# A state space stage whose decays come as running products from one VectorE scan per unit

## The reference, cut to what matters

```python
proj = hidden_states @ W_in.T                    # z | x, B, C | dt
xBC  = silu(causal_conv4(xBC) + conv_b)          # 34 x 128 channels
dt   = softplus(dt + dt_bias);  A = -exp(A_log)
dA   = dt * A                                    # per head and token
Lmat = exp(segsum(dA))                           # L[s,t] = exp(dA[s+1] + ... + dA[t]) for s <= t, else 0
Y_diag = einsum('bclhn,bcshn,bhcls,bcshp->bclhp', C, B, Lmat, x * dt)
y = Y_diag + (states carried over chunks) + D_param * x
g = y * silu(z)
gn = g * rsqrt(mean(g * g) + eps) * norm_w
out = gn @ W_out.T
```

## Time and profile before

| | us |
|---|---|
| median of 3 runs | 4260.26 |
| lowest, highest | 4255.05, 4267.71 |
| span of the profiled execution | 4258.5 |
| this stage, from the first projection of dt to the last layer norm | about 2790 to 3905 |
| distance of two units inside a group | 7.68 |

### The profile page before, as it was taken

The page is one execution under the profiler, slowest core; times in us unless marked ns, Lnnn a source line. Parts: engine busy times, 40 slices in busy tenths (PEclk is TensorE's granted clock), DMA queues, the critical chain, the costliest instruction groups (busy, mean ns, idle before and its releaser), DMA issues. The chain is left out here.

```text
span 4258.5 us, 69394 instructions
## 1 busy us (share of the span) xinstructions
PE 3701.6 (87%) x25058; PEld 2241.4 (53%) x25074; DVE 3141.8 (74%) x6932; ACT 1987.5 (47%) x4723; POOL 970.5 (23%) x1237
## 2 busy tenths in 40 slices
PE   7799999998863868698999989869999999997985
PEld 3466665665642436554555555635555555554543
DVE  7798988987668665624556568768888888886678
ACT  4466666665521423212333334336556565563345
POOL 2433312334202000000111122033323233233220
PEclk9999999999985989898999989989999999997897
DMA  2222222222110000020000000300000000001000
GB/s 68 67 66 63 59 66 58 70 67 47 40 43 28 5 22 2 1 73 21 1 1 1 1 31 2 123 1 1 1 1 1 1 1 1 1 1 48 1 2 20
DMA packets 220834, 118.00 MB, mean 28 GB/s; under 512 B 115536, under 2 KB 213456, under 8 KB 219408
## 3 DMA queue, kind: packets, MB, share of 16 engines
q1 hardware_dynamic: 220496, 113.57, 9.6%
HBM read 98.81 MB, written 14.68 MB: 27 GB/s over the span
## 5 line engine op out<-in xcount | busy, mean ns | idle before, releaser
L305 PE MATMUL ps<-xT,min 128*128 128x512 f32 (+1 forms) x1072 | 534.7, 627 | 7.5 <-DVE mZ L3316 5.2
L3321 DVE SCALAR_TENSOR_TENSOR macc<-ps,mcw,macc 128x508 f32<-128x508 f32 (+2 forms) x408 | 302.9, 742 | 146.4 <-ACT macc L3245 136.8
L3259 ACT ACTIVATE mE<-ps,mcol 128x128 f32<-128x128 f32 x1024 | 291.4, 371 | 8.0 <-PE ps L3159 1.0
L305 PEld LDWEIGHTS ps<-xT,min 128*128 128x128 f32 (+1 forms) x1072 | 182.8, 191 | 190.9 <-issue 181.3
L3407 POOL TENSOR_TENSOR mE<-mE,mCB 128x512 f32<-128x512 f32 x128 | 163.7, 1279 | 481.4 <-ACT mE L3259 481.4
L3189 PE MATMUL ps<-mwo,macc 128*128 128x256 f32 x1024 | 245.9, 383 | 18.9 <-DVE macc L3355 18.9
L2919 ACT ACTIVATE hE<-ps 128x512 f32<-128x512 f32 x256 | 139.0, 595 | 220.5 <-PE ps L2881 220.5
L3414 POOL TENSOR_TENSOR mSQ<-mSQ,mtn 128x512 f32<-128x512 f32 x128 | 163.5, 1277 | 257.8 <-ACT mtn L3263 257.8
L2255 ACT ACTIVATE lP<-ps,lm 128x128 f32<-128x128 f32 x256 | 90.6, 366 | 266.1 <-DVE lm L2315 266.1
L3189 PEld LDWEIGHTS ps<-mwo,macc 128*128 128x128 f32 x1024 | 185.8, 191 | 47.1 <-DVE macc L3355 25.5
L2949 DVE TENSOR_REDUCE hMX<-ps 128x2 f32<-128x512 f32 x256 | 158.9, 684 | 56.9 <-PE ps L2860 56.8
(11 more groups left out here) (604 smaller groups left out, 8981.2 us busy)
## 6 DMA issues: line engine op xcount, KB each, us to landing
dwk<-in_L_attn_Wk SPq DMA_DIRECT2D x64, 128.0 KB, 2.3
dwq<-in_L_attn_Wq SPq DMA_DIRECT2D x64, 128.0 KB, 2.3
dwv<-in_L_attn_Wv SPq DMA_DIRECT2D x64, 128.0 KB, 2.4
dwg<-in_L_attn_Wg SPq DMA_DIRECT2D x64, 128.0 KB, 2.4
dwo<-in_L_attn_Wo SPq DMA_DIRECT2D x64, 128.0 KB, 2.6
min<-in_m_in SPq DMA_DIRECT2D x2, 4096.0 KB, 18.5
d_N<-dNT SPq DMA_DIRECT2D x256, 16.0 KB, 1.5
dTT<-d_TT SPq DMA_DIRECT2D x256, 16.0 KB, 1.9
```

Of the source, the lines that this page charges most:

```text
L305: t = pe.matmul(out, w[:, j, :], self.c.xT[:, j, blk(g, 512)], start=j == 0, stop=j == 1)
L3259: x = act.activation(self.E[s][:, e, blk(j)], bank(4 + e)[:, blk(j)], ACT.Exp, bias=self.col[:, 4 * g + j, 0, 2 * i + e:2 * i + e + 1])
L3321: x = dve.scalar_tensor_tensor(out=acc[:, :, 3 - j:T], in0=p[:, :, 0:T - 3 + j], scalar=self.cw[:, i, j:j + 1], in1=acc[:, :, 3 - j:T], op ...
```

## The change

Only the stage `Scan` changes, and `rsqrt` is cut in two so that a step can begin in its middle.

- ScalarE makes the decay of a single step, exp(dt * A), once for all heads (two instructions, `decay(n)`), with a zero at each block's first token, and SP writes it to DRAM (`m_decay`). For each unit SP reads the two heads' 1024 numbers back into all 128 partitions (512 KB, tile `mE`, four buffers).
- One VectorE scan of 1024 columns a unit (`decay`) forms state = state * step + identity along each row: zero up to the diagonal, 1 on it, then the products of the steps. This is L without exponentials or mask. One VectorE multiply of 1024 columns (`em`) applies B.C to both heads.
- silu is ScalarE's own function for z and x; the factors of one half go.
- The multiply by dt after the turn goes to ScalarE (eight copies of 64 columns with a scale), the copy of B.C goes to ScalarE, the gating goes from VectorE to GpSimd.
- In `order()`, the steps stand differently, and a group's end is spread over more slots. `acc` alternates between banks 0, 1 and 4, 5 by group.

```diff
+        self.before(sp)
+        sp.dma_start(self.id8[:, :, :], self.ins["c_ident"].unsqueeze(1).broadcast_to([128, 8, 128])).then_inc(self.dma[9], 16)
+        for u in range(-1, 128):
+            if u in (-1, 3):
+                n = u // 3 if u > 0 else 0
+                sp.wait_ge(*self.sc.at(n + 1))
+                sp.dma_start(self.decd[2 * n:2 * n + 2].rearrange("e h t -> (e h) t"), self.chain[n][2]).then_inc(self.dma[3 + n], 16)
+            if u in (0, 64):
+                sp.wait_ge(self.dma[3 + u // 64], 16)
+            if u >= 0:
+                g, i = divmod(u, 32)
+                if u >= 4:
+                    sp.wait_ge(*self.y.at(u - 3))
+                rows = self.decd[g, 2 * i:2 * i + 2, :].rearrange("h t -> (h t)").unsqueeze(0).broadcast_to([128, 1024])
+                sp.dma_start(self.E[u % 4][:, :, :].rearrange("p e t -> p (e t)"), rows).then_inc(self.dma[5 + u % 4], 16)
...
-        for t in range(len(seq) + 6):
-            for step, q in (("z", t), ("e0", t - 1), ("x", t), ("e1", t - 1), ("sq", t - 3), ("tr", t - 1), ("acc", t - 3), ("x2", t), ("y", t - 2),
-                            ("close", t - 3), ("stats", t - 4), ("scale", t - 5)):
+        for t in range(len(seq) + 8):
+            for step, q in (("yd", t - 3), ("x2", t - 1), ("em", t - 1), ("z", t), ("x", t), ("close", t - 4), ("cb", t - 1), ("decay", t),
+                            ("tr", t - 1), ("taps", t), ("sq", t - 3), ("acc", t - 3), ("y", t - 2), ("sums", t - 4), ("stats", t - 5),
+                            ("rsqrt", t - 6), ("scale", t - 7)):
...
+            act.activation(g4(u)[:, :, 1:T], g4(x)[:, :, 1:T], ACT.Exp, scale=self.ah[:, 1:2]).then_inc(*self.sc.up)
...
-                act.activation(self.Z[s][:, :], bank(2), ACT.Tanh, scale=0.5).then_inc(*self.zt.up)
+                act.activation(self.Z[s][:, :], bank(2), ACT.Silu).then_inc(*self.zt.up)
...
+                act.activation(out, self.acc[s][:, :], ACT.Silu).then_inc(*self.xs.up)
...
-                    x = act.activation(self.E[s][:, e, blk(j)], bank(4 + e)[:, blk(j)], ACT.Exp, bias=self.col[:, 4 * g + j, 0, 2 * i + e:2 * i + e + 1])
-                x.then_inc(*self.ex.up)
+                    for e in range(2):
+                        h = slice(128 * j + 64 * e, 128 * j + 64 * e + 64)
+                        x = act.activation(self.tn[s][:, h], bank(6)[:, h], ACT.Copy, scale=self.col[:, 4 * g + j, 2 * i + e:2 * i + e + 1])
+                x.then_inc(*self.xd.up)
...
+            elif step == "decay":
+                if u == 0:
+                    dve.wait_ge(self.dma[9], 16)
+                dve.wait_ge(self.dma[5 + u % 4], 16 * (u // 4 + 1))
+                E = self.E[u % 4][:, :, :].rearrange("p e t -> p (e t)")
+                dec = own(dve.tensor_tensor_scan(E, E, self.id8[:, :, :].rearrange("p b t -> p (b t)"), 0.0, ALU.mult, ALU.add))
+            elif step == "em":
+                dve.wait_ge(own.sem, dec)
+                dve.wait_ge(*self.cb.at(g + 1))
+                E = self.E[u % 4][:, :, :]
+                dve.tensor_tensor(E, E, bc(self.CB[g % 2][:, :, :].rearrange("p b t -> p (b t)"), 2), ALU.mult).then_inc(*self.em.up)
+            elif step == "yd":
                 dve.wait_ge(*self.y.at(u + 1))
...
+            elif step == "yd":
+                pool.wait_ge(*self.yd.at(u + 1))
+                pool.wait_ge(*self.zt.at(u + 1))
+                pool.tensor_tensor(self.acc[s][:, :], self.acc[s][:, :], self.Z[s][:, :], ALU.mult).then_inc(*self.ys.up)
```

More of the change, by code:

```diff
@@ L3059, in buffers @@
[L3059 to L3063, removed]
@@ L3064, in buffers @@
-        self.zs, self.cv, self.xs, self.cb, self.m1, self.xd, self.ys = (
-            v("z", 128), v("conv", 136), v("silu", 136), v("cb", 4), v("m", 128), v("xd", 128), v("y", 128))
-        self.sq0, self.m0, self.sqa = p("sq0", 4), p("m", 128), p("sq", 128)
+        self.dtx, self.sc, self.cols = v("dt_sum", 2), s("decay", 2), s("dt_cols", 2)
+        self.aexp, self.won, self.summed, self.smv = s("a", 1), p("wo", 1), v("summed", 4), v("mean", 4)
+        self.zm, self.xm, self.cbm, self.tr, self.y, self.accd, self.sm = (
+            t("z", 128), t("x", 136), t("cb", 4), t("turn", 128), t("y", 128), t("acc", 128), t("sum", 4))
@@ L3079, in order @@
                 g, i = seq[q]
-                if step == "x2" and t < 3:
-                    yield "chain", t, 0, 0, 0
-                if i < 32 and (step not in ("close", "stats", "scale") or i == 31) or step in ("x", "x2"):
+                if step in ("x", "taps", "x2"):
                     yield step, q, units[q], g, i
-                elif i == 33 and step == "e0":
-                    yield "cb", q, units[q], g, i
-                if step == "x" and t == 0:
-                    yield "parts", 0, 0, 0, 0
-                elif step == "x2" and t == 2:
-                    yield "parts", 1, 0, 0, 0
+                elif step == "cb":
+                    if i == 33:
+                        yield step, q, units[q], g, i
+                elif step in ("close", "sums", "stats", "rsqrt", "scale"):
+                    if i == 31:
+                        yield step, q, units[q], g, i
+                elif i < 32:
+                    yield step, q, units[q], g, i
+                if (step, t) in (("x", 0), ("taps", 2)):
+                    yield "parts", t // 2, 0, 0, 0
     def gone(self, q):
@@ L3283, in chain @@
                 then(dve.reciprocal(d, d))
-            elif k == 1:
+            else:
                 then(dve.tensor_tensor(d, d, e, ALU.mult))
@@ L3357, in vector @@
             elif step == "close":
+                dve.wait_ge(*self.sm.at(g + 1))
+                dve.tensor_scalar(self.sw[:, 4:8], bank(6)[:, 0:4], 1.0 / 4096, 1e-5, ALU.mult, ALU.add).then_inc(*self.smv.up)
+            elif step == "sums":
                 sw = self.sw
-                dve.wait_ge(*self.sm.at(g + 1))
+                dve.wait_ge(*self.smv.at(g + 1))
+                r = c.rsqrt_rest(dve, own, [sw[:, blk(n, 4)] for n in range(3)])
                 dve.wait_ge(*self.accd.at(u + 1))
-                r = c.rsqrt(dve, own, bank(6)[:, 0:4], 1e-5, [sw[:, blk(n, 4)] for n in range(3)], scale=1.0 / 4096)
@@ L3368, in vector @@
                 dve.wait_ge(*self.summed.at(g + 1))
-                last = c.moments(dve, own, [(c.R[:, j, :], 0) for j in range(4)], c.st, c.rsq, 1e-5)
+                last = c.moments_of(dve, own, [(c.R[:, j, :], 0) for j in range(4)], c.st)
+            elif step == "rsqrt":
+                dve.wait_ge(own.sem, last)
+                last = c.rsqrt_of(dve, own, c.st, c.rsq, 1e-5)
             elif step == "scale":
```

218 lines of the change are left out of this document (68 added, 150 removed).

## The result

| | before | after |
|---|---|---|
| median of 4 runs, us | 4257.66 | 4186.04 |
| lowest, highest | 4244.98, 4267.71 | 4183.97, 4205.47 |
| span of the profiled execution | 4258.5 | 4182.2 |

The ratio of the means is 0.9844, with a 95% interval of 0.9817 to 0.9871: the change makes the kernel 1.6% faster. The forecast was 4207, the spans differ by 76.3 us where it said 52. Step by step that comes to the following (the prediction's own steps, from the starts of instructions in the two first traces; the intervals from entry 6 to the last are divided into 123 periods and the rest, which are the group ends).

What follows compares the result with a forecast made beforehand. TensorE bounds the kernel at 7.68 us a unit; the bound was to move to VectorE. Units -41, beginning -17, group ends +6, stage's end 0 sum to -52 from 4258.5: 4206.5, forecast 4207 us, range 4160 to 4265.

Steps and rivals of the forecast that it cites:

- TensorE's floor: TensorE per unit: the decays' 0.66 us leave it and nothing is added, 7.68 to 7.02 us.
- VectorE's sum: VectorE per unit: taps, yd, em, scan 6.2 us plus 1.1 lost to GpSimd, 7.3; gain 0.33 a unit, 41 us.
- The gate's hold: GpSimd's gate comes between em and scan and costs VectorE 1.1 us a unit, bounds 0.2 and 1.27.
- The sum of squares beside the taps: GpSimd's second instruction each unit starts 5.1 to 5.7 us into the slot, beside VectorE's taps, and costs nothing.
- The beginning: Stage start until entry 6's taps: eight scans and the decays' spreading gone, 17 us less, bounds 8 and 20.
- The group ends: Three ends at 18.8 us instead of 16.8, VectorE's norm work showing: 6 us more, bounds -15 and +15.
- The stage's end: After the last units: GpSimd's longer gate and eight copies against a shorter VectorE list, 0 us, bounds -4 and +4.
- Rival 1: Units: gate costs only 0.2 us, VectorE stays hidden, TensorE sets 7.02; kernel 4160 us, chance 0.12.
- Rival 2: Units: VectorE starts the scan straight behind em, ahead of the gate; unit 7.6, kernel 4237 us, chance 0.08.
- Rival 3: Every unit's em waits for a late sum of squares: 1.1 us more, unit 8.45, 4342 us; chance 0.14 including milder form.
- its milder form: Units: the scan takes its upper end, 2.74 us; unit 7.85, kernel 4268 us, within a shared chance of 0.14.
- Rival 4: Units: decays arrive late from DRAM, 512 KB a unit at 70 GB/s; kernel about 4250 us, chance 0.06.

Runs made afterwards that it cites:

- the gate on VectorE: Changed kernel with the gating multiply moved from GpSimd to VectorE, between em and the scan: median 4126.36 us, ratio to before 0.9688, unit 6.82 us.
- the identity in PSUM: Changed kernel with one pair of banks for acc, plus the scan's identity operand in PSUM instead of SBUF: stage 1369.5 us against 1430.8, unit 6.82.
- a narrow gate: Changed kernel with GpSimd's gate multiplying only 32 of 512 columns, all waits kept: stage 1342.3 us, unit 6.82 us.
- the three sums: Changed kernel with two more unread 512-column GpSimd additions ahead of each sum of squares: stage 1570.6 us, unit 7.62, later 9.2.
- the decays not read again: Changed kernel reading decays from DRAM for the first four units only: whole run 4201.1 us, stage 1410.5 us, unit 7.26.

## Why the prediction was right, point by point

**TensorE's floor**: mis-sized. The prediction took 0.66 out of 7.68 and got 7.02; the kernels in which TensorE sets the pace run at 6.82. It had overlooked that the decays' instructions also separated z from x, which costs 0.20 us more. In the changed kernel this is hidden, since VectorE's 7.26 lies above both; it shows up once the gate is out of the way. With the gate on VectorE the units give 123 x 0.435 = 53.5 us, the group ends 9.0, the stage's end 7.4 and the beginning 1.0, of 70.9 in all.

**VectorE's sum**: right, and it carries the result. Forecast 2.22 + 0.65 + 1.13 + 2.2 + 1.1 = 7.3, with 0.05 added; measured 2.18 + 0.66 + 1.13 + 2.20 + 1.08 = 7.25. The scan's 2.2, worked out from four short ones, is 2.28 as a length and 2.20 as a distance to the next instruction. The 0.05 for unseen waits doesn't exist, and the taps and the hold are 0.04 and 0.02 shorter than taken: the term is -51.8 instead of -41 because 0.42 us a unit were gained and not 0.33.

**The gate's hold**: right. 1.1 forecast, 1.08 measured; it doesn't depend on the waits around it, since the identity in PSUM removes it with the gate's waits as they were. The Trainium skill, SBUF — State Buffer, section Who interferes with whom, has the port held for the whole instruction. The gate alone is recorded as 1.27 long and the scan loses 1.08, so the full 1.27 that the prediction derived from the page was 0.19 too high here.

**The sum of squares beside the taps**: right. It starts 5.5 us after yd (forecast 5.1 to 5.7) and ends 1.1 before the next em.

**The beginning**: right in kind, -22.0 for -17, 2 outside the bounds of 8 and 20. From dt of the first half to the taps of entry 6 were 62.9 us before, 41.0 after; I had computed 43.4 and then taken 2 us off the gain for TensorE's slow clock. That reserve wasn't needed: the granted clock of this stretch was 0.89, against 0.79 in the kernel before. The decays came in time: the first scan starts at 2811.76, straight behind taps.

**The group ends**: +7.6 for +6 (+6.5 and +8.6 in the other two traces), and this agreement is luck. The forecast of 18.8 us an end counted 10 us of norm work and 4.4 of taps, which would all show because VectorE is the bound, and about 4 of waiting; that is 18.4, not 18.8. From yd of the eleventh unit of group 0 to that of group 1 the windows view of the changed kernel has (first line; columns as in the earlier trace rows):

```profile
2901.81:3154.15 252.34, 235.84 (x1177) 141.14 (x1176) 238.04 (x239) 136.84 (x389) 116.68 (x65) 0.98 0.19 67
3083.80:3089.50 5.70, 5.67 (x25) 4.15 (x25) 5.59 (x9) 1.26 (x2) 2.47 (x1) 0.50 0.00 0
```

32 units at 7.185 busy us make 229.9 of VectorE's 238.04. So of the 20.1 us of this end 8.1 are added work, two taps included, and 12 are waits; TensorE stands for 16.5 us in this stretch, some 5 of them in the 32 units' usual 0.17 each. At a group's end neither engine is the bound. The waits view of VectorE from 2996 to 3125 says what it waits for (us in total, times, longest):

```profile
DVE macc L3307 <- ACT macc L3242: 5.0, 5, 2.0
DVE macc L3325 <- PE ps L3169: 4.7, 3, 3.6
DVE msw L3329 <- PE ps L3190: 1.4, 1, 1.4
```

One long wait there costs TensorE twice:

```profile
3083.83 3.78 PE L3181 MATMUL ps<-mwo,macc 128*128 128x256 f32 x8 [3.64 <-POOL macc L3369]
```

After 3.64 us without work `acc` takes 3.78 us instead of 1.99 and the `y` behind it 1.98 instead of 1.09, at a granted clock of 0.50, the 1.2 GHz level (second line of the windows view). Against this stands the second pair of banks, which the forecast had put into the bounds and not into the sum. Without it the ends would have cost 26.4 us in the mean instead of 20, and the term would have been +27.

**The stage's end**: +3.8, +2.6 and +0.4 in three traces of the changed kernel, between the forecast 0 and the bound of 4.

**The rivals.** Rival 1 (VectorE hidden) is not what happened; it is what the kernels with a narrow gate or a scan that isn't held become, and with 6.82 it is better than its price. Rival 2 (the scan goes ahead of the gate) doesn't hold in the units: 115 of the 128 gates are 2.2 us long. Five of the rest meet no VectorE work that holds them (1.3 us), and three come when a scan without em ahead of it already runs, and stand behind it (3.2 us). That leaves 113 gates that came during em with the scan straight behind: 108 went ahead of the scan, and 5 went behind it (4.3 us). One of these five in the changed kernel's timeline:

```profile
3108.79 4.32 POOL L3369 TENSOR_TENSOR macc<-macc,mZ 128x512 f32<-128x512 f32 x1 [2.89 <-DVE macc L3325]
...
3109.76 2.28 DVE L3317 TENSOR_TENSOR_SCAN mE<-mE,mid 128x1024 f32<-128x1024 f32 x1
...
3113.16 3.62 PE L3181 MATMUL ps<-mwo,macc 128*128 128x256 f32 x8 [3.59 <-POOL macc L3369]
```

em began at 3108.63, so gate, em and scan start at the same distances as in a normal unit, and yet the scan goes first. Here rival 2 is real, and it is part of the group ends' cost: TensorE waits 3.59 us. All five lie in the first five units of a group, and so do the 4 to 6 such gates in each other trace with this gate and scan as they are (the three sums apart). Not every gate there goes behind, and what decides it isn't shown by any run and stays open. Rival 3 is real, as the three sums show, but 1.1 us away, and its milder form fell with the scan's 2.28. Rival 4 fell with the decays not read again.

## What to carry to other kernels

When work moves between engines, price what it does to the instructions it will lie beside, not only its own length: here a multiply of 0.60 us on VectorE was cheaper than the same multiply on idle GpSimd, which cost VectorE 1.08. The scan beside GpSimd kept its pace with one of its two operands in PSUM, 2.27 us instead of 3.35; where a VectorE instruction of two tensors must lie beside GpSimd, this is worth a try. And when instructions leave the engine that bounds a loop, take its new floor from how the remaining ones join up, not by subtraction alone. The end of a loop needs its own account of waits: the engine that bounds the middle need not bound the end.

## What the runs showed of the hardware that had not been expected

- A VectorE scan of 1024 columns takes 2.28 us, whether its second operand is in SBUF or PSUM (2.27), against 1.22 for a multiply of 1024. The Trainium skill, DVE: opcode table, instruction layouts, handler registers and perf-mode slots, section Datapath and trigger behaviour, gives the scan half throughput; (2.28 - 0.07) / (1.22 - 0.07) = 1.9 agrees.
- Of a GpSimd and a VectorE instruction that both wait for the same VectorE instruction to end, GpSimd's mostly goes first (108 of 113), but not always (5 of 113, with the same distances of the starts).
- After a wait of 3.64 us TensorE ran at a granted clock of 0.50, and its `acc` took 3.78 us instead of 1.99.
- A VectorE instruction of four columns with a single tensor operand, in SBUF, was held as well: 1.12 us instead of 0.17, until the sum of squares of 3096.20 was done (timeline of the changed kernel). So having a single operand in SBUF isn't always enough to keep VectorE clear of GpSimd; for the scan it was.

```profile
3096.41 1.12 DVE L205 TENSOR_SCALAR rsq<-rsq 128x4 int32<-128x4 int32 x1
3097.57 0.17 DVE L207 TENSOR_SCALAR rsq<-rsq 128x4 int32<-128x4 int32 x1
```

- 73 GB/s of reads, each 4 KB row spread over 128 partitions, cost no time (unit 7.26 us with and without them, stage 1410.5 us without and 1410.5 to 1413.0 with); 512 KB land in 3.6 us, where the prediction had bounded them by 6.5.
